# Layer 1 attention: heads of a group as one run of 304 columns, denominators by matmuls

## What is computed

```python
k = max(1, int(S * SPARSITY))                    # 76
scores = jnp.einsum('bhqd,bhkd->bhqk', Q, K) / math.sqrt(hd)
scores = jnp.where(sparse_mask[:, None, None, :] == 0, -jnp.inf, scores)
attn = jax.nn.softmax(scores, axis=-1)
out = jnp.einsum('bhqk,bhkd->bhqd', attn, V)     # 16 heads of 8
out = out.transpose(0, 2, 1, 3).reshape(B, S, D)
return out @ wo.T + bo
```

## Time and profile before

| | us |
|---|---|
| median of 3 runs | 1462.51 |
| lowest, highest | 1462.06, 1472.13 |
| span of the profiled execution | 1374.5 |
| layer 1 attention in it, about | 864 to 1040 |

### The profile page before, as it was taken

The page is one execution under the profiler, slowest core; times in us unless marked ns, Lnnn a source line. Parts: engine busy times, 40 slices in busy tenths (PEclk is TensorE's granted clock), DMA queues, the critical chain, the costliest instruction groups (busy, mean ns, idle before and its releaser), DMA issues. The chain is left out here.

```text
span 1374.5 us, 42283 instructions
## 1 busy us (share of the span) xinstructions
PE 1090.5 (79%) x17438; PEld 861.6 (63%) x17438; DVE 885.0 (64%) x1752; ACT 696.4 (51%) x1508; POOL 519.0 (38%) x586
## 2 busy tenths in 40 slices
PE   6678888888888876568778579799996469999974
PEld 4457767666667665457667544455554368888862
DVE  4578888888788866810000067798996746666665
ACT  5444444444444435433343285477775456666654
POOL 4322234224422310057777400121111028888761
PEclk9999999999999997789999879799998789999997
DMA  7622222222222003055555540000003136555556
GB/s 203 181 41 42 42 42 43 41 42 42 42 42 42 4 4 77 2 146 157 159 154 164 145 101 1 0 2 1 1 1 71 39 116 183 177 186 182 181 170 190
DMA packets 151311, 118.88 MB, mean 86 GB/s; under 512 B 37552, under 2 KB 128912, under 8 KB 150608
## 3 DMA queue, kind: packets, MB, share of 16 engines
q1 hardware_dynamic: 142032, 97.54, 27.8%
q0 software_dynamic: 9088, 18.63, 4.5%
HBM read 98.18 MB, written 21.00 MB: 87 GB/s over the span
## 5 line engine op out<-in xcount | busy, mean ns | idle before, releaser
L1873 ACT ACTIVATE act_x_m<-ps_h_x_m,fc_bias_x_m 128x256 f32<-128x256 f32 (+1 forms) x480 | 186.6, 449 | 159.9 <-PE ps_h_x_m L1831 151.7
L1831 PE MATMUL ps_h_x_m<-x_T_x_m,fc_x_m 128*128 128x256 f32 (+1 forms) x960 | 207.7, 368 | 4.1 <-issue 1.9
L1831 PEld LDWEIGHTS ps_h_x_m<-x_T_x_m,fc_x_m 128*128 128x128 f32 x960 | 169.6, 200 | 23.6 <-issue 4.3
L867 ACT ACTIVATE probT<-ps_t 128x512 f32<-128x512 f32 (+1 forms) x192 | 103.9, 591 | 158.6 <-PE ps_t L713 158.6
L1981 POOL DMA_INDIRECT x_rows_x_m<-h_dram,token_m x142 | 140.2, 988 | 110.4 <-POOLq L1538 70.6
L1991 POOL DMA_INDIRECT y_dram<-y_x_m,dest_m x142 | 141.1, 994 | 66.8 <-issue 38.9
L1850 PE MATMUL ps_o_x_m<-proj_x_m,act_x_m 128*128 128x128 f32 x1136 | 145.9, 282 | 5.1 <-DVE act_x_m L1895 5.1
L1850 PEld LDWEIGHTS ps_o_x_m<-proj_x_m,act_x_m 128*128 128x128 f32 x1136 | 138.2, 198 | 6.0 <-DVE act_x_m L1895 5.9
L1917 DVE TENSOR_TENSOR y_x_m<-ps_o_x_m,out_rows_m 128x256 f32<-128x256 f32 (+1 forms) x40 | 15.8, 394 | 178.5 <-PE ps_o_x_m L1850 178.5
L860 ACT ACTIVATE prob<-prob 128x512 f32<-128x512 f32 (+1 forms) x64 | 81.3, 1271 | 87.6 <-DVE prob L815 87.6
L713 PE MATMUL ps_t<-ident,prob 128*128 128x128 f32 (+1 forms) x768 | 106.9, 284 | 6.6 <-ACT probT L867 5.1
(11 more groups left out here) (296 smaller groups left out, 2052.1 us busy)
## 6 DMA issues: line engine op xcount, KB each, us to landing
q_spread<-q_dram SPq DMA_DIRECT2D x256, 64.0 KB
fc_x_m<-L_ffn_c_fc SPq DMA_DIRECT2D x40, 256.0 KB
proj_x_m<-L_ffn_c_proj SPq DMA_DIRECT2D x40, 256.0 KB
fc_x_m<-L_ffn_Wi SPq DMA_DIRECT2D x40, 256.0 KB
fc_x_m<-L_ffn_Wg SPq DMA_DIRECT2D x40, 256.0 KB
proj_x_m<-L_ffn_Wo SPq DMA_DIRECT2D x40, 256.0 KB
got_m<-y_dram SPq DMA_DIRECT2D x32, 256.0 KB, 5.0
h_dram<-h_rows_m SPq DMA_DIRECT2D x16, 256.0 KB, 2.3
```

Of the source, the lines that this page charges most:

```text
L867: act.activation(probT[0:ks, store(m, ch), :, (2 * j + s) % 4, :], ps_t[0:ks, t % 2, :].rearrange("p (g c) -> p g c", g=GROUPS), ACT.Copy) ...
L1831: m = pe.matmul(ps_h[:, l, g, f % 2, 0:w], fc[:, slot, l, f * P:(f + 1) * P], x_T[:, slot % 2, 0:w], start=True, stop=True)
L1873: m = act.activation(out[:, slot % 2, f, 0:w], ps_h[:, l, g, f % 2, 0:w], ACT.Tanh if l else ACT.Gelu, scale=0.5 if l else 1.0, bias=fc_bi ...
```

## The change

A group's four heads are taken as one run of 4 x 76 = 304 columns, which is cut into chunks of 128, 128 and 48. The transposes of a round become 12 (three chunks of four groups), and a PSUM buffer now holds one chunk of all four groups. The values need the same layout, heads one below the other over the partitions, so ScalarE writes the gathered values as rows (`v_rows`) and SP brings them by six small transfers a batch (`flat_pieces`) into `v_flat`, whose zeros GpSimd writes once. The last chunk has 48 rows; the rest of its part of `probT` is cleared once, and the matmul takes all 128.

The row sums on VectorE, their inverse, the widening on GpSimd, the two transposes and ScalarE's copy go. In their place a table of ones, `head_ones` (1 where a row belongs to a head, for that head's 8 columns), is multiplied with the turned probabilities, 12 matmuls of 256 columns right behind the values. They give the sums already spread over the channels, and VectorE takes the reciprocal of all 128 x 256 of them from PSUM before the product.

```diff
+FLAT = 4 * KEPT
+CHUNKS = -(-FLAT // P)
+def flat_pieces():
+    pieces = []
+    for h in range(4):
+        r = 0
+        while r < KEPT:
+            c, at = divmod(KEPT * h + r, P)
+            n = min(KEPT - r, P - at)
+            pieces.append((h, r, n, c, at))
+            r += n
+    return pieces
...
+        @block.sync
+        def _(sp):
+            sp.wait_ge(values_clear, 1)
+            for b in range(B):
+                sp.wait_ge(v_ready, b + 1)
+                wait(sp, gated, b - 2)
+                for h, r, n, c, at in pieces:
+                    sp.dma_start(view(v_flat[at:at + n, b % 3, c, :, :], HD * h, [[4 * HD, 4], [1, HD]]),
+                                 view(v_rows[r:r + n, b % 2, :], HD * h, [[4 * HD, 4], [1, HD]])).then_inc(v_in[b % 2], 16)
...
-                for p in groups:
-                    t = 4 * m + p
+                for c in parts:
+                    t = CHUNKS * m + c
                     wait(pe, copied, t - 1)
-                    for h in range(4):
-                        x = pe.transpose(ps_t[0:KEPT, t % 2, h * P:(h + 1) * P], prob[:, m % 2, p, h, :], k.ident[:, :])
+                    for p in range(4):
+                        x = pe.transpose(ps_t[0:flat_rows(c), t % 2, p * P:(p + 1) * P],
+                                         view(prob[:, m % 2, p, 0, :], P * c, [[1, flat_rows(c)]]), k.ident[:, :])
...
+                pe.wait_ge(v_in[b % 2], 16 * len(pieces) * (b // 2 + 1))
                 wait(pe, gated, b)
-                for h in heads:
+                for c in parts:
                     for p in range(4):
-                        pe.matmul(ps_y[group(p), 0, :], v_diag[:, b % 3, 4 * p + h, :], probT[:, b % 2, p, h, :],
-                                  start=h == 0, stop=h == 3, skip_group_check=True)
+                        pe.matmul(ps_y[group(p), 0, :], v_flat[:, b % 3, c, p, :], probT[:, b % 2, c, p, :],
+                                  start=c == 0, stop=c == CHUNKS - 1, skip_group_check=True)
             def denominators(b):
-                pe.wait_ge(inv_spread, b + 1)
-                for u in range(2):
-                    x = pe.transpose(ps_y[:, 1, u * P:(u + 1) * P], inv_wide[:, b % 2, u, :, :], k.ident[:, :])
+                if b == 0:
+                    pe.wait_ge(ones_ready, 1)
+                for c in range(CHUNKS):
+                    for p in range(4):
+                        x = pe.matmul(ps_y[group(p), 1, :], head_ones[:, c, :, :], probT[:, b % 2, c, p, :],
+                                      start=False, stop=c == CHUNKS - 1, skip_group_check=True)
...
-                    turn(m - 1, (2, 3))
+                    turn(m - 1, (2,))
...
-                    values(b - 1, (2, 3))
+                    values(b - 1, (2,))
                     denominators(b - 1)
...
             def normalize(b):
-                dve.wait_ge(inv_copied, b + 1)
+                dve.wait_ge(y_done, b + 1)
+                dve.reciprocal(inv_y[:, :], ps_y[:, 1, :]).then_inc(inv_ready, 1)
+                dve.wait_ge(inv_ready, b + 1)
                 dve.tensor_tensor(y_T[:, b % 2, :], ps_y[:, 0, :], inv_y[:, :], ALU.mult).then_inc(y_ready, 1)
...
-                if exists(m - 1):
-                    row_sums(m - 1)
-                if u == 0 and 1 <= b <= B:
-                    invert(b - 1)
...
             def split_values(b):
                 act.wait_ge(k_ready, b + 1)
-                act.activation(view(v_diag[:, b % 3, 0, :], 0, [[16 * HD, 4], [5 * HD, 4], [1, HD]]),
-                               view(ps_g[0:KEPT, :], v_at, [[4 * HD, 4], [HD, 4], [1, HD]]), ACT.Copy).then_inc(v_ready, 1)
+                if b >= 2:
+                    act.wait_ge(v_in[b % 2], 16 * len(pieces) * (b // 2))
+                act.activation(v_rows[:, b % 2, :], ps_g[0:KEPT, v_at:v_at + C], ACT.Copy).then_inc(v_ready, 1)
...
-            def copy_inv(b):
-                act.wait_ge(y_done, b + 1)
-                act.activation(inv_y[:, :], ps_y[:, 1, :], ACT.Copy).then_inc(inv_copied, 1)
...
+            pool.memset(probT[:, :, CHUNKS - 1, :, :], 0.0).then_inc(probs_clear, 1)
+            step = Chain(pool, pool_step)
+            step(pool.memset(head_ones[:, :, :, :], 1.0))
+            for c in range(CHUNKS):
+                step(pool.affine_select(out=head_ones[:, c, :, :], in_=head_ones[:, c, :, :], compare_op=ALU.is_ge, fill=0.0,
+                                        base=P * c, pattern=[[-KEPT, 4], [0, HD]], channel_multiplier=1))
+                step(pool.affine_select(out=head_ones[:, c, :, :], in_=head_ones[:, c, :, :], compare_op=ALU.is_ge, fill=0.0,
+                                        base=KEPT - 1 - P * c, pattern=[[KEPT, 4], [0, HD]], channel_multiplier=-1))
```

More of the change, by code:

```diff
@@ L1224, in sparse_attention_phase @@
         k_diag = sb("k_diag", [P, 2, 4, KEPT])
-        v_diag = sb("v_diag", [KEPT, 3, H, 4 * HD])
+        v_rows = sb("v_rows1", [KEPT, 2, C])
+        v_flat = sb("v_flat1", [P, 3, CHUNKS, 4, 4 * HD])
         prob = sb("prob1", [P, 2, 4, 4, KEPT])
         neg_max = sb("neg_max1", [P, 2, 4, 4])
-        probT = sb("probT1", [KEPT, 2, 4, 4, T])
-        row_sum, row_inv = sb("row_sum1", [P, 2, 2, H]), sb("row_inv1", [P, 2, 2, H])
-        inv_wide, inv_y = sb("inv_wide1", [P, 2, 2, H, HD]), sb("inv_y1", [P, T])
+        probT = sb("probT1", [P, 2, CHUNKS, 4, T])
+        head_ones = sb("head_ones", [P, CHUNKS, 4, HD])
+        inv_y = sb("inv_y1", [P, T])
         y_T, upd = sb("y_T1", [P, 2, T]), sb("upd1", [P, 2, T])
@@ L1236, in sparse_attention_phase @@
         selected, gathered, k_ready, v_ready = sem("selected"), sem("gathered"), sem("k_ready4"), sem("v_ready4")
[L1237 to L1240, removed]
+        score, maxed, subbed, expd = (sem(n) for n in ("score1", "maxed1", "subbed1", "expd1"))
+        turned, copied, ones_ready, pool_step = (sem(n) for n in ("turned1", "copied1", "ones_ready", "pool_step1"))
+        y_done, inv_ready, y_ready, projd = (sem(n) for n in ("y_done1", "inv_ready1", "y_ready1", "projd1"))
+        gated, added = sem("gated1"), sem("added1")
+        values_clear, probs_clear = sem("values_clear1"), sem("probs_clear1")
+        v_in = [sem(f"v_in1_{i}") for i in range(2)]
+        pieces = flat_pieces()
         block = ctx.enter_context(nc.Block())
@@ L1385, in exp, with copy @@
                 act.activation(p_, p_, ACT.Exp).then_inc(expd, 1)
-            def copy(m, groups):
+            def copy(m):
                 b, u = m // 2, m % 2
-                for p in groups:
-                    t = 4 * m + p
+                for c in range(CHUNKS):
+                    t, n = CHUNKS * m + c, flat_rows(c)
                     act.wait_ge(turned, t + 1)
-                    act.activation(probT[:, b % 2, p, :, u * P:(u + 1) * P],
-                                   ps_t[0:KEPT, t % 2, :].rearrange("p (h q) -> p h q", h=4), ACT.Copy).then_inc(copied, 1)
-            def copy_inv(b):
-                act.wait_ge(y_done, b + 1)
-                act.activation(inv_y[:, :], ps_y[:, 1, :], ACT.Copy).then_inc(inv_copied, 1)
+                    act.activation(probT[0:n, b % 2, c, :, u * P:(u + 1) * P],
+                                   ps_t[0:n, t % 2, :].rearrange("p (g q) -> p g q", g=4), ACT.Copy).then_inc(copied, 1)
             def gate(b):
@@ L1403, in gate @@
                                bias=a.gate_bias[:, b:b + 1]).then_inc(gated, 1)
-            act.wait_ge(cleared, 1)
             split_values(0)
+            act.wait_ge(probs_clear, 1)
             for m in range(ROUNDS + 3):
                 b, u = m // 2, m % 2
-                if u == 0 and b >= 2:
-                    copy_inv(b - 2)
                 if exists(m - 1):
-                    copy(m - 1, (0, 1))
-                    copy(m - 1, (2, 3))
+                    copy(m - 1)
                 if exists(m):
```

29 lines of the change are left out of this document (9 added, 20 removed).

## The result

The changed kernel takes 1503.62 us in the median of four runs (1493.26 to 1513.55), the kernel before 1462.63 us: slower by a ratio of 1.0275, 95% interval 1.0217 to 1.0332. 1495 us was forecast.

What follows compares the result with a forecast made beforehand. Each layer 1 attention batch was taken as a latency chain, then TensorE's own work, with the reciprocal lengthening the chain. 1462.5 + 21.5 (batches, start, tail) + 11 (clock) = 1495 us; range 1480 to 1510.

Steps and rivals of the forecast that it cites:

- The batch at full clock: Layer 1 attention: a batch takes 6.60 + 5.16 = 11.76 us against 10.29, with a reciprocal of 1.80 us.
- Transposes, values and denominators: TensorE's second half: transposes 1.00 and 0.56 us, values of chunks 0, 1 1.00, chunk 2 values with denominators 1.87.
- The clock: TensorE's 2.3 us wait before the projection lowers the granted clock: 7 falls at 1.6 us, +11 us.
- half of the batches: Of 14 batches, half run 3.4 us at half clock from the start of TensorE's second half; bounds none or all.
- The start: First two batches, without normalizing: shorter rounds of transposes and an earlier exponential gain about 1 us; setting up is hidden.
- The tail: After the last scores: earlier projection -0.3, last values and denominators +0.5, reciprocal +1.4; together +1.6 us.
- The value transfers: SP's six small transfers a batch, 0.31 us each to issue, are hidden unless six take above 11.8 us.
- 88 us around the span: Time outside the profiled 1374.5 us span, in the median of 1462.5 us, was taken to stay.
- The clock holds (1): Rival: same latency chain in layer 1 attention, but no fall of the clock, 1484 us; chance 0.17.
- Reciprocal of 2.0 us and a fall in nearly every batch (2): Rival: same chain in layer 1 attention, longer reciprocal and more clock falls, 1509 us; chance 0.12.
- Transfers (3): Rival: value transfers set the pace, six taking 14 us make a batch 14 us, some 1514 us; chance 0.03.
- Not slower (4): Rival: reciprocal at VectorE's ordinary rate, 0.4 us, batch 10.36 us, whole 1462 to 1465 us; chance 0.05.

Runs made afterwards that it cites:

- Experiment 2: Changed kernel with 16 transposes of the identity added in TensorE's wait for y_T, batches 2 to 15: 1405.8 us, ratio 1.016 to the kernel before.
- experiment 7: Changed kernel with ScalarE's wait for the cleared probabilities moved ahead of the first split of values: 1430.18 us in one run.
- experiment 1: Changed kernel with the reciprocal taking 32 of the 256 columns, the others set to ones: 1388.12 us, ratio 1.0023 to the kernel before.
- experiment 3: Changed kernel with the projection moved behind the odd scores on TensorE, values and ScalarE's gate moved too: 1397.51 us, ratio 1.0065 to the kernel before.
- experiment 4: Changed kernel's flat layout and value transfers, with denominators as in the kernel before: 1370.43 us, ratio 0.9893 to the kernel before.

## Why the prediction came out as it did

The direction was right, and so was the mechanism: the reciprocal in the chain, the wait for y_T, the falls of the clock behind it. The range of 1480 to 1510 us holds 1503.62. The stage grew by 41.2 us where 32.5 stood in the sum; nearly all of what is missing is in the clock and at the start. The terms, one by one:

- **The batch at full clock** was put at 6.60 + 5.16 = 11.76 us and is 6.55 + 5.17 = 11.72. The reciprocal was taken as 1.80 and is 1.75, by the row of 16 lanes in the earlier trace rows nearly to the nanosecond (1745 for 1740); the number of lanes makes no difference, and the upper end of 2.0, drawn from the short reciprocals, was too high. The Trainium skill's repeat count of 8 (VectorE: DVE Perf Modes, Walkthrough: the 8-slice pipeline in each mode) gave an estimate of 2.13 us at the page's clock; the trace does not agree, at 1.75 us or 6.8 ns an element. Over the batches this term was +20.9 and is 13 x 1.43 + 1.79 = +20.4.
- **Transposes, values and denominators.** Each was right to 0.05 us: in the timeline 1.02 + 1.00 + 0.55 + 1.87 for 1.00 + 1.00 + 0.56 + 1.87.
- **The clock** is where the sum fell short. 7 falls at 1.6 us were expected, +11; it was 11 falls at about 1.6 us. Ten of them are in the 13 full batches: 36.0 - 20.4 = 15.6 us. The eleventh is in the tail. The wait itself was right (2.28 for 2.3), and so was the price of one fall; the step that failed is "half of the batches". More rows would not have mended it: of the eleven waits of 1.64 to 3.08 us at full clock in layer 0's experts, in the trace of the kernel before, five were followed by a fall, one of 1.67 us among them, and one of 2.98 us was not. What those rows do not have is the loop: there the waits come unevenly, here one in every batch, and then four of five are followed by a fall. That the count lay at the edge of what was forecast (4 to 11) is partly luck. Experiment 2 shows the size of the term.
- **The start** was -1 and is +2.0. Two things are in it. The load of the table went behind the subtraction (experiment 7), which I had not seen in the order of the waits; and TensorE was at half clock for longer than before: the mean granted clock from first gather to the scores of batch 2 is 0.62 for 0.73. How much of that belongs to the change is open: it is 0.70 in experiment 2, whose program is the same up to there.
- **The tail** was +1.6 and is +3.2, of which about 1.6 is the eleventh fall.
- **The value transfers** were hidden, as said, though an issue costs more than the 0.31 us of the earlier trace rows. SP's issues of the changed kernel, ns min/median/max:

```profile
L1286 SPq DMA_DIRECT2D v_flat<-v_rows x96: 624/794/927, 919.1 to 1107.0; - x96
```

  Six are 4.8 us a batch of a queue that has nothing else to do.
- **"88 us around the span"** was wrong. The changed kernel's runs show spans 1.9 us below their times; the 88 us of the kernel before are a difference between executions, perhaps between two chips. The sum did not suffer, since it was one of differences within the stage, and the stage shows the same 41 us in both traces.
- **The rivals.** The clock holds (1): it did not, except where the wait was filled, shortened or moved away (experiments 2, 1 and 3). Reciprocal of 2.0 us and a fall in nearly every batch (2): its clock half came nearly true, its reciprocal not. Transfers (3): refuted by experiments 1 and 4. Not slower (4): experiment 1 gives that case by its short reciprocal, at +2.3 us, for the forecast of 0 to 2.

The sum of the stage as measured: 2.0 + 20.4 + 15.6 + 3.2 = 41.2 us.

## What to carry to other kernels

Work taken off an engine that has slack is worth nothing, and what takes its place is priced by where it stands: a 1.75 us reciprocal between two steps of a chain of latencies stood in every batch at its full length and left the stage 41 us above the kernel before, while with the same reciprocal and the projection moved it is 11 us above. When a change has two parts, price each for itself; here one was worth -15 us and the other, alone, +67, and the sum hid both. And waits of 1.84 and 2.28 us on TensorE had a second price in the clock here, which a few useless transposes in the wait showed and removed.

## What the runs showed that was not expected

- A reciprocal has a price per element of about 6.8 ns: 256 a lane take 1745 ns on 128 lanes and 1740 ns on 16; the row sum of 1216 elements, which it was to save, takes 1.41 us.
- Falls of the clock do not simply follow the length of the wait. Waits of 2.28 us (3.17 the last) were followed by 3.4 us at half clock in 11 of 14 batches in both traces, always four in a row with one spared between; waits of 0.88 us in none; waits of 1.84 us in some, and there two stretches of 17 us came. Why they were so long is open.
- With two waits ahead of the first exponential, its table load ran only behind the subtraction, 1.3 us too late. In the trace it is a load with an idle time of 4.18 us before it, ended by VectorE.
- More work made the kernel faster: the 16 added transposes a batch took 17.2 us off the stage.
